# Weighing the values once per graph for all twelve heads, with the projections laid out anew over the slots, in a two-layer graph attention kernel

## The reference

```python
h = relu(layernorm(x))                      # layer 0
q, k, v = h @ Wq + bq, h @ Wk + bk, h @ Wv + bv          # 12 heads of 32
s = q @ k.T / sqrt(32) + beta * adj;  s = where(adj > 0, s, -9e15)
x = x + softmax(s) @ v
h = relu(layernorm(x))                      # layer 1
q, k, v = h @ Wq.T, h @ Wk.T, h @ Wv.T + bv
o = softmax(q @ k.T * 384**-0.5 + adj) @ v
x = x + o @ Wo.T + bo
```

## Time and profile before

| | us |
|---|---|
| median of 3 runs (2566.4 to 2567.91) | 2566.66 |
| the profiled execution | 2566.11 |
| its span, first to last instruction | 2564.3 |
| PE busy (94%) | 2414.5 |
| DVE busy (81%) | 2073.9 |
| ACT busy (80%) | 2051.0 |
| POOL busy (28%) | 719.5 |

### The profile page before, as it was taken

One profiled execution on the slowest core, in us unless ns is written; L12 is line 12 of the kernel. 1 busy time (PEld: TensorE's weight loads), 2 busy tenths in 40 slices (PEclk: granted clock), 3 DMA queues, 4 the chain that ended last, 5 costly groups with the idle time before them and its releaser, 6 DMA issues. The chain is left out here.

```text
span 2564.3 us, 75830 instructions
## 1 busy us (share of the span) xinstructions
PE 2414.5 (94%) x20736; PEld 1436.2 (56%) x20736; DVE 2073.9 (81%) x10570; ACT 2051.0 (80%) x7816; POOL 719.5 (28%) x1159
## 2 busy tenths in 40 slices
PE   5899999999999999999999999999999999999987
PEld 3555555555555555555555555555555555555554
DVE  5788887888888888878888878888778888788866
ACT  4788888888888888888788888888887888888876
POOL 1322332222322223323223223223222233222221
PEclk9899999999999999999999999999999999999998
DMA  6333433433334333334333343333343343343321
GB/s 180 96 90 96 108 86 102 106 94 104 95 94 108 95 96 101 93 102 112 87 98 104 88 103 102 96 101 98 95 108 89 95 108 88 101 106 92 89 69 42
DMA packets 256436, 251.21 MB, mean 98 GB/s; under 512 B 23632, under 2 KB 256080, under 8 KB 256080
## 3 DMA queue, kind: packets, MB, share of 16 engines
q1 hardware_dynamic: 256080, 248.08, 36.5%
HBM read 71.83 MB, written 25.17 MB: 38 GB/s over the span
## 5 line engine op out<-in xcount | busy, mean ns | idle before, releaser
L455 ACT ACTIVATE probs<-neg,neg_max 128x128 f32<-128x128 f32 x3072 | 1187.5, 391 | 105.3 <-issue 64.8
L455 ACT ACTIVATION_READ_ACCUMULATOR probs<-neg,neg_max 128x1 f32 x3072 | 584.2, 190 | 0.0
L500 ACT ACTIVATE probs_t<-pt_bank 128x512 f32<-128x512 f32 x768 | 448.6, 584 | 97.0 <-PE pt_bank L742 95.4
L719 PE MATMUL job_bank<-h_hi,w_hi 128*128 128x512 f16 x1152 | 441.8, 384 | 61.5 <-DVE part_lo L601 43.4
L742 PE MATMUL pt_bank<-ident,probs 128*128 128x128 f32 x3072 | 462.5, 273 | 4.1 <-ACT probs_t L500 3.8
L742 PEld LDWEIGHTS pt_bank<-ident,probs 128*128 128x128 f32 x3072 | 381.7, 141 | 128.8 <-ACT probs L455 10.2
L719 PE MATMUL job_bank<-h_lo,w_hi 128*128 128x512 f16 x1152 | 441.4, 383 | 0.0
L719 PE MATMUL job_bank<-h_hi,w_lo 128*128 128x512 f16 x1152 | 440.4, 382 | 0.0
L543 DVE CUSTOM_DVE_ANT_0 neg<-score_bank,adj 128x128 f32<-128x128 f32 x1536 | 353.3, 286 | 1.2 <-issue 1.2
L543 DVE CUSTOM_DVE_ANT_0 neg<-score_bank,bias 128x128 f32<-128x128 f32 x1536 | 353.3, 286 | 0.0
L400 POOL TENSOR_TENSOR rstd<-shift_var,minus_half 128x1 f32<-128x1 f32 x256 | 140.3, 548 | 755.2 <-DVE shift_var L577 753.9
(11 more groups left out here) (59 smaller groups left out, 3789.2 us busy)
## 6 DMA issues: line engine op xcount, KB each, us to landing
stack<-part_hi SPq DMA_DIRECT2D x768, 128.0 KB, 3.2
stack<-part_lo SPq DMA_DIRECT2D x384, 128.0 KB, 3.3
x_norm<-in_x SPq DMA_DIRECT2D x32, 768.0 KB, 4.7
x_res<-in_x SPq DMA_DIRECT2D x32, 768.0 KB, 4.6
out_x<-result SPq DMA_DIRECT2D x128, 192.0 KB, 1.9
adj<-in_adj SPq DMA_DIRECT2D x64, 256.0 KB, 3.2
stack<-in_L_gnn_Wq SPq DMA_DIRECT2D x2, 576.0 KB, 7.0
stack<-in_L_gnn_Wk SPq DMA_DIRECT2D x2, 576.0 KB, 8.0
```

Source lines behind the costliest of these rows:

```text
L455: last = act.activation(probs[c % 2][:, h, :], neg[c % 2][:, h, :], ACT.Exp, bias=neg_max[:, b, first + h:first + h + 1], scale=-1.0, accu ...
L500: act.activation(probs_t[c % 2][:, :, :].rearrange("p h q -> p (h q)"), pt_bank[:, :], ACT.Copy).then_inc(probs_t_ready, 1)
L719: last = pe.matmul(to, stationary, moving, start=(m == 0), stop=(m == MATMULS - 1))
```

## The change

`weigh_values` no longer runs once per chunk with four heads, but once per graph with twelve, in the slot in which the last of the graph's three chunks used to be weighed (slots 1, 4, 7 and 10). `probs_t` grows from four heads to twelve per buffer, and its two buffers now alternate by graph; `pv_done` counts graphs (`GROUP` per unit) instead of chunks. The number of matmuls, copies and waits of each kind on DVE and ACT stays the same. `PROJ` gets new numbers. Summed up slot by slot, the old rows reach 7 14 21 27 34 41 48 54 63 72 81 90 and 5 13 21 25 32 40 45 54 66 72 81 90, the new ones 4 8 17 21 25 35 42 48 58 70 77 90 and 9 15 24 33 36 46 48 52 64 69 75 90. A job ends in the slot in which the sum reaches nine times its number plus nine.

```diff
-PROJ = ((7, 7, 7, 6, 7, 7, 7, 6, 9, 9, 9, 9), (5, 8, 8, 4, 7, 8, 5, 9, 12, 6, 9, 9))
+PROJ = ((4, 4, 9, 4, 4, 10, 7, 6, 10, 12, 7, 13), (9, 6, 9, 9, 3, 10, 2, 4, 12, 5, 6, 15))
...
-        probs_t = [sb(f"probs_t{b}", [P, HC, NODES]) for b in range(2)]
+        probs_t = [sb(f"probs_t{b}", [P, HEADS, NODES]) for b in range(2)]
...
-                        if some(n - 2):
-                            act.wait_ge(pv_done, n - 2)
-                        act.activation(probs_t[c % 2][:, :, :].rearrange("p h q -> p (h q)"), pt_bank[:, :],
-                                       ACT.Copy).then_inc(probs_t_ready, 1)
+                        b, first = c // KC, c % KC * HC
+                        if first == 0 and some(u.n * GROUP + b - 1):
+                            act.wait_ge(pv_done, u.n * GROUP + b - 1)
+                        act.activation(probs_t[b % 2][:, first:first + HC, :].rearrange("p h q -> p (h q)"),
+                                       pt_bank[:, :], ACT.Copy).then_inc(probs_t_ready, 1)
...
-                if some(u.n * SLOTS - SLOTS):
-                    dve.wait_ge(pv_done, u.n * SLOTS - SLOTS)
+                if some(u.n * GROUP - GROUP):
+                    dve.wait_ge(pv_done, u.n * GROUP - GROUP)
...
-                        dve.wait_ge(pv_done, chunk(u, b * KC + KC - 1))
+                        dve.wait_ge(pv_done, u.n * GROUP + (b + 1))
...
-            def weigh_values(u, c):
-                n = chunk(u, c)
-                b = c // KC
-                pe.wait_ge(probs_t_ready, n)
-                if c % KC == 0:
-                    pe.wait_ge(v_ready, u.n * GROUP + (b + 1))
+            def weigh_values(u, b):
+                pe.wait_ge(probs_t_ready, chunk(u, b * KC + KC - 1))
+                pe.wait_ge(v_ready, u.n * GROUP + (b + 1))
...
-                for h in range(HC):
-                    f = P * (c % KC) + HEAD * h
-                    last = pe.matmul(o_bank[HEAD * h:HEAD * (h + 1), P * (c % KC):P * (c % KC + 1)],
-                                     v32[u.parity][:, b, f:f + HEAD], probs_t[c % 2][:, h, :], start=True, stop=True)
+                for h in range(HEADS):
+                    d, f = HEAD * (h % HC), P * (h // HC)
+                    last = pe.matmul(o_bank[d:d + HEAD, f:f + P], v32[u.parity][:, b, HEAD * h:HEAD * (h + 1)],
+                                     probs_t[b % 2][:, h, :], start=True, stop=True)
...
-                    u, c = unit_of_chunk(p, s - 2)
+                    u, b = finished(p, s, 2)
                     if u is not None:
-                        weigh_values(u, c)
+                        weigh_values(u, b)
```

More of the change, by code:

```diff
@@ L743, in turn_probs @@
                 last.then_inc(probs_turned, 1)
-            def weigh_values(u, c):
-                n = chunk(u, c)
-                b = c // KC
-                pe.wait_ge(probs_t_ready, n)
-                if c % KC == 0:
-                    pe.wait_ge(v_ready, u.n * GROUP + (b + 1))
[L752 to L759, removed]
-                for h in range(HC):
-                    f = P * (c % KC) + HEAD * h
-                    last = pe.matmul(o_bank[HEAD * h:HEAD * (h + 1), P * (c % KC):P * (c % KC + 1)],
-                                     v32[u.parity][:, b, f:f + HEAD], probs_t[c % 2][:, h, :], start=True, stop=True)
+            def weigh_values(u, b):
+                pe.wait_ge(probs_t_ready, chunk(u, b * KC + KC - 1))
+                pe.wait_ge(v_ready, u.n * GROUP + (b + 1))
+                if u.layer == 0 and (b > 0 or (isinstance(u.n, int) and u.n == 1)):
+                    pe.wait_ge(o_taken, u.group * GROUP + b)
+                elif u.layer == 0 and some(u.group * GROUP - GROUP):
+                    pe.wait_ge(o_norm_ready, u.group * GROUP - GROUP)
+                elif u.layer == 1 and (b > 0 or (isinstance(u.n, int) and u.n == UNITS - 1)):
+                    pe.wait_ge(o_norm_ready, u.group * GROUP + b)
+                elif u.layer == 1:
+                    pe.wait_ge(o_taken, u.group * GROUP + 2 * GROUP)
+                for h in range(HEADS):
+                    d, f = HEAD * (h % HC), P * (h // HC)
+                    last = pe.matmul(o_bank[d:d + HEAD, f:f + P], v32[u.parity][:, b, HEAD * h:HEAD * (h + 1)],
+                                     probs_t[b % 2][:, h, :], start=True, stop=True)
                 last.then_inc(pv_done, 1)
```

## The result

| | before | after |
|---|---|---|
| median of the runs, us | 2566.93 | 2675.56 (2672.54 to 2676.55) |
| ratio to before, 95% interval | | 1.042 [1.041, 1.043] |
| span of the profiled execution, us | 2564.3 | 2674.5 |
| granted clock over the span | 0.99 | 0.98 |

A forecast was written before the change was run, and what follows sets the result against it. It took TensorE to bound T4, VectorE T3 and T5, both T1; +1.03 + 0.91 + 0 - 0.60 + 0.47 = +1.81 us per turn, about 31 turns, +56 us, gave 2622 us, range 2545 to 2665.

The forecast's parts named there:

- T1: Layer-1 phase, inverse-sum transposes of slot 7 to those of slot 10, 9.92 us: +1.03 from a wait in slot 8.
- T2: From slot 10's inverse-sum transposes to the last take of v in slot 11, 2.90 us: predicted +0.91.
- T3: From slot 11's last take of v to slot 1's inverse-sum transposes in the layer-0 phase, 7.84 us: predicted 0.
- T4: From slot 1's inverse-sum transposes to o_t of slot 11, layer-0 phase, 27.13 us, called TensorE's stretch: predicted -0.60.
- T5: From o_t of slot 11 to the next slot-7 inverse-sum transposes, 30.33 us, VectorE busy 29.07: predicted +0.47.
- Rival B: TensorE alone bounds the kernel, so the 93 us saved come off: 2473 us; chance 0.17.
- The block: Weighing twelve heads together as six waves was to take 0.99 us in place of 3 x 0.45 = 1.35.
- rival C: The merged block is no cheaper than three: +1.4 us per turn in T1 and T4, 2667 us; chance 0.11.
- Nine matmuls later: Step of T2 in slot 11: VectorE takes the last v at 1030.3, after 1028.65 + 8 x 0.163 + 0.33.
- rival A: Handovers are looser and job 7's wait in slot 8 costs nothing: +0.1 us per turn, 2570 us; chance 0.22.
- old wait in slot 2: In T4, the wait for job 0's low part was to go, as job 2 starts in slot 4: -0.54 us.
- wait in slot 6: In T4, a new wait of job 4 on job 2's low part: about +0.06 us.

The follow-up runs named there:

- e4_far8_after: The changed kernel with VectorE's layer-1 reduction over far taken over 8 of 128 columns of each head; 2547.97 us, ratio 0.993.
- e7_early_bias: Merged block with old table, plus VectorE's next mask and bias built in slots 9 and 10 of the layer-0 phase instead of 11; 2505.68 us.
- e2_block_only: The changed kernel with the old PROJ table, so only the merged block; 2535.08 us, ratio 0.987 to before.
- e6_three_moved: The changed kernel with three projections moved from slot 3 to slot 4 of the layer-0 phase; 2667.56 us, ratio 1.039.
- e11_best: Merged block, old table with eight layer-0 projections moved from slot 10 to 11, slots 3 and 4 split 8 and 5, mask and bias early; 2505.25 us.
- e9_new0: The merged block with the new table row for the layer-0 phase only, old row for layer 1; 2588.01 us, ratio 1.008.
- e10_new1: The merged block with the new table row for the layer-1 phase only, old row for layer 0; 2608.31 us, ratio 1.016.
- e3_fill: The changed kernel plus 32 unread TensorE matmuls at the end of slot 7 of the layer-1 phase; 2656.53 us, ratio 1.035.
- e5_two_moved: The changed kernel with two projections moved from slot 8 to slot 7 of the layer-1 phase; 2614.02 us, ratio 1.018.
- e12_mask4: The kernel of e11_best with the next mask built at the end of slot 4 in place of slot 9; 2491.70 us, ratio 0.971.

## Why the prediction was wrong

The turn got 3.84 us longer, not 1.81. By stretch, the difference of 2.03 is T1 +0.65, T2 +0.49, T3 -0.17, T4 +1.07, T5 -0.03.

**What bounds the kernel: right.** T5 is VectorE's (e4_far8_after, e7_early_bias), TensorE's saved time in T3 and T5 became idle time (2.13 us at inverse(7); 1.31 at the scores behind the turn of the loop and 0.91 at inverse(1), where the prediction looked for over 2 us), and e2_block_only, which takes 256 x (3 x 0.45 - 0.89) = 118 us of TensorE's work away, gains 32. Rival B falls with it. That T4 is "TensorE's stretch" was too coarse: its first 6 to 7 us are a chain through four engines (e6_three_moved), and VectorE's room in it is small (e11_best). So a shorter TensorE gave back only a part of its time there.

**The block: right mechanism, the size at its lower bound,** 0.89 for 0.99; rival C falls.

**T5: right,** +0.44 for +0.47; e9_new0 and e10_new1 tie it to the row of the layer-0 phase, where the take of job 7 moved into slot 11.

**T1: the wait was right, the clock was missed.** Without the lower clock T1 grows by 0.95, predicted 1.03. The failed step is that each handover was priced at a full clock throughout. The prediction let TensorE's waits in T5 "come back at a later handover" and put nothing down for them; the idle time itself was hidden, but in 18 of the 26 turns the clock fell behind it, on work that is not hidden. That is 0.73 us per turn, 19 us by e3_fill.

**T2: the mechanism was right, one term was left out.** "Nine matmuls later" left out that the four transposes of the probabilities stand among these nine (row 1069.62): 0.44 us, and T2 is +1.40, not +0.91. The earlier trace rows has no row of slot 11, where they would have been seen; the sum of rival A does count them.

**T4: the step that failed most.** The prediction says "as job 2 starts in slot 4". The new row adds up to 4 8 17 21, so slot 3 holds matmuls 17 to 20, and 18 is the first of job 2. With the terms as measured:

| us | predicted | measured |
|---|---|---|
| nine blocks to three | -1.09 (its terms give -1.08) | -1.38 |
| four projections more, 46 of 512 columns | +0.97 | +0.97 |
| old wait in slot 2 | -0.54 | -0.54 |
| wait in slot 3 | none | +1.08 |
| wait in slot 6 | +0.06 | +0.37 |
| sum | -0.60 | +0.50, the stretch +0.47 |

The miscount alone does not tell the loss: e6_three_moved corrects it and gains 0.08 us, since the chain to `o_lo` would have taken up what the blocks of slots 2 and 3 save. That the saved time would come off in T4 in full was the second error, and the one that counts: with job 2 in slot 4, as the prediction had it, T4 is 27.52 us, +0.39 and not -0.60.

**T3: right in size, not in the reason.** It got 0.17 us shorter in the mean of 26 turns and 0.11 in the 25 with a turn of the loop in it, nearly the predicted 0. What holds it there is the turn of the loop, and not VectorE's list: outside the loop T3 fell by 1.76 us. Why VectorE stands still at the turn, no run tried.

**The number of turns** was taken as 31. The whole difference is 108.6 us, 28.3 times 3.84: what is outside the loop hardly moved. So 31 was too much by a tenth, and it made the miss in the total look smaller than the miss per turn.

**The range** left out 2675 because its top was rival C's lower part, a more costly block. No case in it was a second wait in T4, or a second cost in T1; the errors lay in what the waits bring with them, not in the price of an instruction.

## What to carry to other kernels

Where engines hand over in turn, price a new order stretch by stretch, and within a stretch ask what the next wait would be before counting a saving: e2_block_only kept 32 of the 118 us (256 x 0.46) that its blocks save, and two numbers of a table (e5_two_moved) were worth 61 us. When a table says where work stands, number the items and write down into which slot each waiting one falls: the prediction placed one a slot too late and missed a wait of 1.08 us, and behind it stood another wait of 1.04 (e6_three_moved). A wait of TensorE that seems hidden still has a price if the clock falls behind it, and once TensorE's list is shorter, the next gain was in relieving VectorE (e7_early_bias, e12_mask4).

## What the runs showed of the hardware

- **The clock fell at short idle times of TensorE.** The four kernels in which it idled 2.10 to 2.13 us ahead of inverse(7), after a stretch with few projections, had the lower level for 3.41 us in 7 to 18 of 26 turns; those with 0.24 to 1.59 us had none. Not every turn of the same kernel had it. Few projections alone did not do it (e4_far8_after has as few, 0.81 us of idle time and no such stretch); whether the idle time alone would was not tried.
- **Twelve heads in four columns of the array cost 0.89 us,** 24 f32 matmuls with 24 weight loads, and four heads 0.45: 0.11 us per further wave of four.
- **The same instruction of VectorE takes 0.42 or 0.98 us.** The mask (128x512, f32) stood at 0.42 in slot 4 and 0.98 in slot 9, where POOL had just started a 1.00 us addition. In e7_early_bias and e11_best, with the mask in slot 9, it took 0.95 to 0.98 us in 60 of 64 executions, each beside that addition; in no other kernel did it take over 0.46. The Trainium skill ("GPSIMD Engine Reference", 1. Specifications) says that GpSimd shares its SBUF interfaces with VectorE, and contends with those VectorE instructions that are in a 2-port perf mode or have two SBUF inputs. The rows agree with a contention, but they do not show the mask's mode, and no run varied POOL alone, so the cause is not shown. From start to start the mask took 0.90 us in slot 9 and 0.34 in slot 4.
